# A graph layer in fp32 halves on one Trainium2 core: three row blocks instead of two share the features while these are made

## The chip, the cores and the metric

The kernel runs on one core of a Trainium2 chip. The metric is the device time of one execution in microseconds (us), as the median of the runs shown. The engines are named as in the profile: PE (matrix products; PEld its weight loads), DVE (vector), ACT (scalar), POOL (GpSimd) and SP (the queue that issues most transfers). PE's sums land in eight accumulator banks of 128 x 512 fp32, the tensor `banks`.

## The reference

```python
h = relu(layernorm(x))                      # x 4096 x 256; layernorm without gain or bias, eps 1e-5
deg = sum(adj, axis=1) + 1e-5               # adj 4096 x 4096, dense fp32
out = (adj / deg) @ h @ W_neigh.T + b_neigh + h @ W_self.T + b_self
result = x + relu(out)                      # fp32, 4096 x 256
```

## The kernel before

The 4096 rows of the result are cut into 8 row blocks of 512 (q = 0 to 7). The sum over neighbours is cut into 16 units of 256 columns of `adj` (u = 0 to 15). So there are 128 units, numbered s = 0 to 127 in the order of the table `order` (line 33). Unit (q, u) needs 512 KB of `adj` and the pair u of feature tiles, h of 256 nodes.

Products are made from halves: a value is split into a rounded high part and the rest. PE forms hi·hi, lo·hi and hi·lo for each unit, 12 matmuls of 128 x 512 (lines 573 to 575), which add up over 16 units in the two banks of the row block (`MAIN`).

What each engine does, each in its own program order:

- **SP** loads unit s into slot s % 4 of the ring `adj_raw` (line 173). It first waits until unit s - 4 has been split by ACT and DVE and, where DVE adds it to the row sums, until that is done. Behind the load of some units it issues a pair of x tiles (`load_x`, line 163).
- **ACT** makes the high part of unit s ("hi", line 292). At unit `make_at[p]` it also makes h of pair p (`make_h`, line 295), which waits for POOL's `shift` and `rstd`, and at `split_at[p]` its high part.
- **DVE** makes the low part of unit s ("lo", line 434), and at unit `norm_at[p]` the mean and variance of pair p ("statistics", lines 397 and 401), for which it waits for that pair's x. Then it adds the unit into `total`, from which the degrees come ("add", line 446; a copy, line 443, for the first of a row block). Before the first unit that uses a pair it makes the low part of its h (line 426).
- **POOL** turns variance and mean of a pair into `rstd` and `shift` with four small operations (lines 214, 216, 225, 222). It also issues 14 transfers that add units of q = 0 and 1 into `total_dma` in memory, so that DVE need not add those (`by_dma`, lines 38 and 239).

The slots of the rings are reused after four units, so hi and lo of unit s also wait until PE has used unit s - 4.

While h is being made, units of row blocks 0 and 1 alternate (units 0 to 31): each new pair of h serves two units. After that a row block is 16 units in a row, with h complete.

For each row block there is a second part. `turn` transposes the block's own h (8 transposes, line 590) into two banks, ACT and DVE split that, and `own_product` (24 matmuls, line 599) multiplies it by W_self. `weigh` multiplies the finished sum by W_neigh (24 matmuls), after ACT and DVE have split it (`product_high`, line 351; `product_low`, line 469). `sum_degrees` (line 623) sums the degrees over partitions with four tiny matmuls, from `sums`, which DVE joins (lines 453 and 458); `degrees` (line 474) and `join_rows` (line 483) on DVE, relu on ACT, and `add_bias` (line 247) and `add_x` (line 253) on POOL finish the rows. At which unit each of these stands in each engine's program is written in tables (lines 45 to 56).

The eight banks: two pairs for the sums of even and odd row blocks, one pair for the small products (`SMALL`), one for the transposed h and the degrees (`TURNED`, `SUMMED`). At the end the last block's rows take banks 4, 5, 0, 1.

Of the kernel before, what the change touches and what calls it, by code (L numbers as in the profile page):

```python
# [5 lines left out]
P = 128  # L6
# [15 lines left out]
def gnn_layer(nc, x, adj, wn, ws, bn, bs, out):  # L22
# [23 lines left out]
    own_at = [36, 47, 57, 66] + [16 * q + 11 for q in range(4, Q)]  # L46
    weigh_at = [38, 49, 59, 68] + [16 * (q + 1) + 2 for q in range(4, Q)]
    degrees_at = [w + 1 for w in weigh_at[:-1]]

    product_at = [32, 42, 52] + [last_unit[q] + 3 for q in range(3, Q)]  # L50
# [4 lines left out]
    split_at = [0, 1, 3] + [2 * p - 1 for p in range(3, PAIRS - 1)] + [2 * PAIRS - 4]  # L55
    sums_at = [38, 45, 54, 64] + last_unit[4:]

    with ExitStack() as ctx:
# [91 lines left out]

        MAIN = [[0, 1], [2, 3]]
        SMALL = [4, 5]
        TURNED = [6, 7]
        SUMMED = 7

        TAIL = [4, 5, 0, 1]

        block = ctx.enter_context(nc.Block())

        @block.sync  # L160
        def _(sp):
# [24 lines left out]
            load_unit(3)  # L186
            load_x(3)
            for s in range(RING, S):
                load_unit(s)
                if s % 2 == 0 and s // 2 + 2 < PAIRS:  # L190
                    load_x(s // 2 + 2)
                if s == 9:
                    sp.dma_start(w_raw[:, :, 0, :], wn).then_inc(s_w, 16)
                if s == 11:
                    sp.dma_start(w_raw[:, :, 1, :], ws).then_inc(s_w, 16)
                if s == 13:
# [12 lines left out]
        def _(pool):  # L209
# [57 lines left out]
            for s in range(S):  # L267
# [3 lines left out]
                for n in range(len(by_dma)):  # L271
                    if s == 5 * n // 2 + 5:
                        add_unit(n)
                for q in range(Q):
                    if s == own_at[q] + 5 and q < Q - 1:
                        add_bias(q)
                    if s == weigh_at[q] + 7 and q < Q - 1:
                        add_x(q)
# [7 lines left out]
        def _(act):  # L286
# [41 lines left out]
            def turned_high(q):  # L328
                if q >= 1:
                    act.wait_ge(s_own, 2 * q)  # L330
                for k in range(KC):
                    act.wait_ge(s_turned, 2 * q + k + 1)
                    nc.scalar.activation(ht_hi[:, k, :], banks[:, TURNED[k], :], ACT.Copy).then_inc(s_hthi, 1)

# [8 lines left out]
            def product_high(q):  # L343
                if q >= 1:
                    act.wait_ge(s_weighed, 2 * q)
                for k in range(KC):
                    if k == 0:
                        act.wait_ge(s_half, q + 1)
                    else:
                        act.wait_ge(s_used, last_unit[q] + 1)  # L350
                    nc.scalar.activation(p_hi[:, k, :], banks[:, MAIN[q % 2][k], :], ACT.Copy).then_inc(s_phi, 1)  # L351

# [10 lines left out]
            for s in range(1, S):  # L363
                split_unit(s)
                for p in range(1, PAIRS):
                    if s == make_at[p]:
                        make_h(p)
                    if s == split_at[p]:
                        split_h(p)
                if s == 29:  # L370
                    act.wait_ge(s_w, 32)
                    nc.scalar.activation(w_hi[:, :, :, :], w_raw[:, :, :, :], ACT.Copy).then_inc(s_whi, 1)
                for q in range(Q):
# [4 lines left out]
                    if s == own_at[q] + 4:  # L378
                        take_own(q)
                    if s == product_at[q]:  # L380
                        product_high(q)
                    if s == weigh_at[q] + 6:
                        relu(q)
# [10 lines left out]
        def _(dve):  # L394
# [65 lines left out]
            def turned_low(q):  # L460
                for k in range(KC):
                    dve.wait_ge(s_hthi, 2 * q + k + 1)
                    nc.vector.tensor_tensor(ht_lo[:, k, :], banks[:, TURNED[k], :], ht_hi[:, k, :].bitcast(F32),
                                            ALU.subtract).then_inc(s_htlo, 1)

            def product_low(q):
                for k in range(KC):
                    dve.wait_ge(s_phi, 2 * q + k + 1)
                    nc.vector.tensor_tensor(p_lo[:, k, :], banks[:, MAIN[q % 2][k], :], p_hi[:, k, :].bitcast(F32),
                                            ALU.subtract).then_inc(s_plo, 1)  # L470

            def degrees(q):
                dve.wait_ge(s_summed, q + 1)
                nc.vector.tensor_scalar(deg[:, 0, :], banks[:, SUMMED, 0:UI], DEG_EPS, None, ALU.add).then_inc(s_deg, 1)  # L474
                dve.wait_ge(s_deg, q + 1)
# [25 lines left out]
            for s in range(2, S):  # L501
                if s < T and (s % 2 == 0 and s < T - 2 or s == T - 3):
                    split_h(order[s][1])
# [4 lines left out]
                if by_vector[s]:  # L508
                    add_unit(s)
                if s == 30:  # L510
                    dve.wait_ge(s_whi, 1)
# [4 lines left out]
                for q in range(Q):  # L516
                    if s == turn_at[q] + 4:
                        turned_low(q)
                    if s == product_at[q]:
                        product_low(q)  # L520
                    if s == sums_at[q]:
                        join_sums(q)
                    if s == weigh_at[q] + 4:
                        degrees(q)
# [17 lines left out]
        def _(pe):  # L542
# [16 lines left out]
            def add_unit(s):  # L559
                q, u = order[s]  # L560
                r = s % RING
                if s < T:
                    pe.wait_ge(s_hlo, u + 1)
                if u == 0 and q >= 2:
                    pe.wait_ge(s_plo, 2 * (q - 1))
                pe.wait_ge(s_lo, s + 1)
                for k in range(KC):
                    bank = banks[:, MAIN[q % 2][k], :]
                    feats = slice(k * P, (k + 1) * P)
# [10 lines left out]
            def turn(q):  # L580
# [3 lines left out]
                else:  # L584
                    pe.wait_ge(s_htlo, 2 * q)
                if q >= 1:
                    pe.wait_ge(s_deg, q)
                for k in range(KC):
                    for t in range(UI):
                        last = nc.tensor.transpose(banks[:, TURNED[k], t * P:(t + 1) * P],  # L590
                                                   h_row[:, t // 2, t % 2, k * P:(k + 1) * P], ident[:, :])
# [22 lines left out]
            def sum_degrees(q):  # L614

                pe.wait_ge(s_sums, q + 1)
                pe.wait_ge(s_htlo, 2 * q + 2)
                if q == 0:
                    pe.wait_ge(s_ones, 1)
                else:  # L620
                    pe.wait_ge(s_deg, q)
                for t in range(UI):
                    last = nc.tensor.matmul(banks[:, SUMMED, t:t + 1], sums[:, t * P:(t + 1) * P], ones[:, :],  # L623
                                            start=True, stop=True)
# [27 lines left out]
            for s in range(1, S):  # L652
# [3 lines left out]
                for q in range(Q):  # L656
                    if s == turn_at[q]:
                        turn(q)
                    if s == own_at[q]:
                        own_product(q)  # L660
                    if s == weigh_at[q]:
                        weigh(q)
# [36 lines left out]
```

## Time and profile before

| | |
|---|---|
| median of 3 runs | 438.15 us (436.0 to 438.83) |
| the profiled execution | 436.03 us |
| its span | 434.0 us |
| PE busy in the span | 419.2 us (97%) |
| DVE busy | 360.0 us (83%) |
| ACT busy | 208.0 us (48%) |
| POOL busy | 113.7 us (26%) |
| moved by transfers | 83.98 MB, mean 194 GB/s |

The span runs from the first to the last instruction that counts; the 2 us between span and time lie around it. PE's busy time is an upper bound, since the ends of its matmuls are modelled and overlap; the step from one start to the next is the surer measure, and the times between a wait and the next start are real.

### The profile page before, as it was taken

What the parts mean: (1) busy time and instruction counts of PE and PEld (TensorE: products, weight loads), DVE (VectorE), ACT (ScalarE), POOL (GpSimd) and SP (SyncE); (2) the same over time, 40 slices, a digit from 0 to 9 for tenths busy, and PEclk for the clock granted to TensorE, in tenths of its full rate; (3) what the DMA queues carried; (4) which work ended last, traced back from release to release, by engine and by line L of the source; (5) the groups of instructions that cost most, each with busy time, mean ns of one, the idle gap of its engine ahead of it and who ended that gap; (6) DMA issues with size and microseconds to landing.
All of it is one profiled execution on the core that took longest, in us unless ns stands there. A gap on an engine that the chain in (4) does not pass through costs nothing.

```text
span 434.0 us, 5622 instructions
## 1 busy us (share of the span) xinstructions
PE 419.2 (97%) x2057; PEld 350.7 (81%) x2057; DVE 360.0 (83%) x421; ACT 208.0 (48%) x267; POOL 113.7 (26%) x107
## 2 busy tenths in 40 slices
PE   7799999988999999999999999999999999999995
PEld 4578877766888888888888888888888888888884
DVE  5688888989899896996797796979878897869934
ACT  4675555556533733734442544435342643426411
POOL 4365676741020303432203202002110302003021
PEclk9989999999999999999999999999999999999999
DMA  8779999999945474465347364545745465453501
GB/s 281 250 236 316 310 308 287 290 233 287 272 152 195 145 231 158 142 225 166 109 136 239 127 209 154 192 145 160 242 141 194 138 205 183 146 194 101 189 2 48
DMA packets 25482, 83.98 MB, mean 194 GB/s; under 512 B 2800, under 2 KB 4336, under 8 KB 25456
## 3 DMA queue, kind: packets, MB, share of 16 engines
q1 hardware_dynamic: 22864, 75.64, 52.0%
q0 software_dynamic: 2016, 7.34, 8.3%
q10 hardware_dynamic: 576, 0.66, 0.5%
q8 instruction: 16, 0.26, 0.3%
q14 instruction: 10, 0.08, 0.1%
HBM read 79.43 MB, written 4.19 MB: 193 GB/s over the span
## 4 chain that ended last, share of the span: by engine, by line
PE 74%; DVE 8%; POOL 8%; ACT 4%; issue 3%; DMA 3%; DVEq 0%; POOLq 0%; ACTq 0%; SPq 0%
PE banks L573 20%; PE banks L574 20%; PE banks L575 20%; PE banks L599 10%; DVE adj_lo L434 3%; POOL rstd L216 3%; POOL shift L225 2%; ACT adj_hi L292 2%; DMA adj_raw<-adj_in 2%; POOL rstd L214 2%; DVE total L446 2%; PE banks L590 2%; PE banks L623 1%; ACT h_row L295 1%; DVE stats L397 1%
## 5 line engine op out<-in xcount | busy, mean ns | idle before, releaser
L573 PE MATMUL banks<-adj_hi,h_hi 128*128 128x512 f32 x508 | 201.5, 397 | 7.6 <-DVE adj_lo L434 6.0
L292 ACT ACTIVATE adj_hi<-adj_raw 128x1024 fp32r<-128x1024 f32 x127 | 133.9, 1057 | 146.9 <-PE banks L575 128.2
L575 PE MATMUL banks<-adj_lo,h_hi 128*128 128x512 f32 x508 | 198.6, 391 | 0.0
L574 PE MATMUL banks<-adj_hi,h_lo 128*128 128x512 f32 x508 | 198.6, 391 | 0.0
L434 DVE TENSOR_TENSOR adj_lo<-adj_raw,adj_hi 128x1024 fp32r<-128x1024 f32 x127 | 167.4, 1318 | 35.4 <-ACT adj_hi L292 34.9
L446 DVE TENSOR_TENSOR total<-total,adj_raw 128x1024 f32<-128x1024 f32 x106 | 131.1, 1237 | 0.0
L573 PEld LDWEIGHTS banks<-adj_hi,h_hi 128*128 128x128 f32 x508 | 95.8, 189 | 31.5 <-issue 10.5
L575 PEld LDWEIGHTS banks<-adj_lo,h_hi 128*128 128x128 f32 x508 | 95.7, 188 | 20.6
L574 PEld LDWEIGHTS banks<-adj_hi,h_lo 128*128 128x128 f32 x508 | 95.9, 189 | 18.4
L253 POOL TENSOR_TENSOR x_sb<-x_sb,own 128x1024 f32<-128x1024 f32 x7 | 29.1, 4161 | 135.3 <-ACT own L355 135.3
L247 POOL TENSOR_TENSOR own<-own,b_sum 128x1024 f32<-128x1024 f32 x8 | 22.6, 2823 | 116.8 <-ACT own L340 116.8
L295 ACT ACTIVATE h_row<-x_sb,shift,rstd 128x256 f32<-128x256 f32 x62 | 32.9, 591 | 32.0 <-POOL shift L222 32.0
L474 DVE TENSOR_SCALAR deg<-banks 128x4 f32<-128x4 f32 x8 | 1.3, 162 | 22.0 <-PE banks L623 22.0
L351 ACT ACTIVATE p_hi<-banks 128x512 fp32r<-128x512 f32 x16 | 9.2, 597 | 20.3 <-PE banks L575 14.1
L599 PE MATMUL banks<-w_hi,ht_lo 128*128 128x256 f32 x64 | 18.1, 283 | 0.0
L599 PE MATMUL banks<-w_lo,ht_hi 128*128 128x256 f32 x64 | 18.1, 283 | 0.0
L599 PE MATMUL banks<-w_hi,ht_hi 128*128 128x256 f32 x64 | 18.1, 282 | 0.0
L216 POOL TENSOR_TENSOR rstd<-rstd,consts 128x2 f32<-128x2 f32 (+1 forms) x17 | 17.3, 1017 | 1.3
L214 POOL TENSOR_TENSOR rstd<-mv,consts 128x2 f32<-128x2 f32 (+1 forms) x17 | 10.5, 617 | 27.2 <-DVE mv L401 27.2
L239 POOL DMA_DIRECT2D total_dma<-adj_in x12 | 10.7, 891 | 22.0 <-PE banks L575 17.7
L599 PE MATMUL banks<-w_hi,p_lo 128*128 128x256 f32 x56 | 15.8, 283 | 0.0
L599 PE MATMUL banks<-w_lo,p_hi 128*128 128x256 f32 x56 | 15.8, 283 | 0.0
(65 smaller groups left out, 288.0 us busy)
## 6 DMA issues: line engine op xcount, KB each, us to landing
adj_raw<-adj_in SPq DMA_DIRECT2D x127, 512.0 KB, 4.0
total_dma<-adj_in POOLq DMA_DIRECT2D x14, 512.0 KB, 7.9
x_sb<-x_in SPq DMA_DIRECT2D x14, 256.0 KB, 6.0
rows_out<-x_sb SPq DMA_DIRECT2D x7, 512.0 KB, 5.0
adj_raw<-adj_in SPq DMA_DIRECT2D x2, 256.0 KB, 4.5
x_sb<-x_in ACTq DMA_DIRECT2D x1, 256.0 KB, 4.2
w_raw<-w_neigh SPq DMA_DIRECT2D x1, 256.0 KB, 5.4
w_raw<-w_self SPq DMA_DIRECT2D x1, 256.0 KB, 6.1
```

The costliest lines, as they stand in the source:

```text
L214: nc.gpsimd.tensor_tensor(rstd[:, cols], mv[:, cols, 1], consts[:, 0, 0:n], ALU.add).then_inc(s_rstd, 1)
L216: nc.gpsimd.tensor_tensor(rstd[:, cols], rstd[:, cols], consts[:, 1, 0:n], ALU.pow).then_inc(s_rstd, 1)
L247: nc.gpsimd.tensor_tensor(own[:, :, :], own[:, :, :], b_sum[:, :, :].broadcast_to([P, UI, F]), ALU.add) \
L253: nc.gpsimd.tensor_tensor(x_sb[:, rows, :], x_sb[:, rows, :], own[:, :, :], ALU.add).then_inc(s_final, 1)
L292: nc.scalar.activation(adj_hi[:, r, :, :], adj_raw[:, r, :, :], ACT.Copy).then_inc(s_hi, 1)
L295: return nc.scalar.activation(slot, x_sb[:, t, :], ACT.Relu, bias=shift[:, t:t + 1], scale=rstd[:, t:t + 1])
L434: nc.vector.tensor_tensor(adj_lo[:, r, :, :], adj_raw[:, r, :, :], adj_hi[:, r, :, :].bitcast(F32), ALU.subtract).then_inc(s_lo, 1)
L446: nc.vector.tensor_tensor(total[:, q % 3, :, :], total[:, q % 3, :, :], adj_raw[:, s % RING, :, :], ALU.add).then_inc(s_add, 1)
L573: nc.tensor.matmul(bank, h_hi[:, j, feats], adj_hi[:, r, a, :], start=first, stop=False)
L574: nc.tensor.matmul(bank, h_lo[:, j, feats], adj_hi[:, r, a, :], start=False, stop=False)
L575: done = nc.tensor.matmul(bank, h_hi[:, j, feats], adj_lo[:, r, a, :], start=False, stop=last)
L599: last = nc.tensor.matmul(bank, m[:, k, cols], w[:, k, which, :], start=(n == 0), stop=(n == len(terms) - 1))
```

## The change

Row blocks 0, 1 and 2 now take turns while h is made (units 0 to 47), so each new pair of h serves three units. Three sums are open at once; with row block 3 it is four, so `MAIN` gives banks 0 to 7 to row blocks 0 to 3 and reuses banks 2, 3 and 6, 7 afterwards. The small products then take banks 0 and 1, which are free once row block 0 has been split, and the transposed h takes 0 and 1 for two blocks and 4 and 5 later. The turns, own products and weights of all blocks therefore stand behind unit 48. The tables for x loads, statistics, making and splitting h, `by_dma` transfers and the second part of each block are rewritten for that; `by_dma` names the same 14 units.

```diff
-    order = [(s % 2, s // 2) for s in range(2 * U - 4)] + [(q, u) for q in range(2) for u in range(U - 2, U)]
-    order += [(s // U, s % U) for s in range(2 * U, S)]
+    order = [(s % 3, s // 3) for s in range(3 * U - 6)] + [(q, u) for q in range(3) for u in range(U - 2, U)]
+    order += [(s // U, s % U) for s in range(3 * U, S)]
...
-    turn_at = [32, 43, 53, 62] + [16 * q + 8 for q in range(4, Q)]
+    turn_at = [50, 61, 71, 78, 86, 96, 104, 120]
+    degrees_at = [49, 60] + [w + 1 for w in weigh_at[2:]]
...
-    norm_at = [0, 0, 2, 3] + [2 * p - 4 for p in range(4, PAIRS)]
-    make_at = [0, 1, 3] + [2 * p - 2 for p in range(3, PAIRS - 1)] + [2 * PAIRS - 5]
+    norm_at = [0, 0, 2, 4] + [3 * p - 5 for p in range(4, PAIRS)]
+    make_at = [0, 1] + [3 * p - 3 for p in range(2, PAIRS - 1)] + [first_use[-1] - 2]
...
-        MAIN = [[0, 1], [2, 3]]
-        SMALL = [4, 5]
-        TURNED = [6, 7]
-        SUMMED = 7
-        TAIL = [4, 5, 0, 1]
+        MAIN = [[0, 1], [2, 3], [4, 5], [6, 7], [2, 3], [6, 7], [2, 3], [6, 7]]
+        EARLIER = [None, None, None, None, 1, 3, 4, 5]
+        SMALL = [0, 1]
+        TURNED = [[0, 1]] * 2 + [[4, 5]] * (Q - 2)
+        SUMMED = [0, 0] + [5] * (Q - 2)
+        TAIL = [0, 1, 2, 3]
...
-                if s % 2 == 0 and s // 2 + 2 < PAIRS:
-                    load_x(s // 2 + 2)
+                if s % 3 == 2 and 5 < s and (s + 4) // 3 < PAIRS:
+                    load_x((s + 4) // 3)
...
-                pool.wait_ge(s_used, 5 * n // 2 + 2)
+                pool.wait_ge(s_used, 3 * n + 2)
...
-                    if s == weigh_at[q] + 4:
+                    if s == degrees_at[q] + 3:
                         degrees(q)
...
-                if q >= 1:
+                if q == 0:
+                    pe.wait_ge(s_deg, 1)
+                elif q == 1:
+                    pe.wait_ge(s_joined, 1)
+                    pe.wait_ge(s_deg, 2)
+                else:
+                    pe.wait_ge(s_plo, 6)
                     pe.wait_ge(s_deg, q)
```

How instructions move, at three places. First DVE, while h is made. Before, from the statistics of pair 10 to those of pair 11 (units 16 to 18; `adj_lo` is lo, `total` the add, `h_lo` the low part of h, `mv` ends the statistics):

```order
L397 BN_STATS stats<-x_sb 128x6 [waits x_pair_loaded10]
L397 BN_STATS stats<-x_sb 128x6
L401 BN_AGGR mv<-stats 128x2 [waits stats_done]
L401 BN_AGGR mv<-stats 128x2
L446 TENSOR_TENSOR total<-total,adj_raw 128x1024 [waits unit_added]
L434 TENSOR_TENSOR adj_lo<-adj_raw,adj_hi 128x1024 [waits adj_unit_used,adj_hi_ready]
L426 TENSOR_TENSOR h_lo<-h_row,h_hi 128x512 [waits h_hi_ready]
L434 TENSOR_TENSOR adj_lo<-adj_raw,adj_hi 128x1024 [waits adj_unit_used,adj_hi_ready]
L397 BN_STATS stats<-x_sb 128x6 [waits x_pair_loaded11]
```

Now, from the statistics of pair 6 to those of pair 7 (units 13 to 16); between those of pairs 7 and 8 stand two more adds, one ahead of the first lo and one behind the second:

```order
L400 BN_STATS stats<-x_sb 128x6 [waits x_pair_loaded6]
L400 BN_STATS stats<-x_sb 128x6
L404 BN_AGGR mv<-stats 128x2 [waits stats_done]
L404 BN_AGGR mv<-stats 128x2
L437 TENSOR_TENSOR adj_lo<-adj_raw,adj_hi 128x1024 [waits adj_unit_used,adj_hi_ready]
L449 TENSOR_TENSOR total<-total,adj_raw 128x1024 [waits unit_added]
L429 TENSOR_TENSOR h_lo<-h_row,h_hi 128x512 [waits h_hi_ready]
L437 TENSOR_TENSOR adj_lo<-adj_raw,adj_hi 128x1024 [waits adj_unit_used,adj_hi_ready] x2
L400 BN_STATS stats<-x_sb 128x6 [waits x_pair_loaded7]
```

The statistics of neighbouring pairs were two units apart and are now three apart.

Second PE, around the first `turn`. Before, behind unit 32:

```order
L573 MATMUL banks<-adj_hi,h_hi 128x512
L574 MATMUL banks<-adj_hi,h_lo 128x512
L575 MATMUL banks<-adj_lo,h_hi 128x512
L590 MATMUL banks<-ident,h_row 128x128 [waits ident_ready,h_again_ready]
L590 MATMUL banks<-ident,h_row 128x128 x7
L573 MATMUL banks<-adj_hi,h_hi 128x512 [waits adj_lo_ready]
```

Now, behind unit 50:

```order
L578 MATMUL banks<-adj_hi,h_hi 128x512
L579 MATMUL banks<-adj_hi,h_lo 128x512
L580 MATMUL banks<-adj_lo,h_hi 128x512
L602 MATMUL banks<-ident,h_row 128x128 [waits degree_step_done,ident_ready,h_again_ready]
L602 MATMUL banks<-ident,h_row 128x128 x7
L578 MATMUL banks<-adj_hi,h_hi 128x512 [waits adj_lo_ready]
```

The turn now also waits for `degree_step_done`, the first step of `degrees` on DVE (L477 below). There it stands behind lo and add of unit 52, here from the lo of unit 51 on:

```order
L437 TENSOR_TENSOR adj_lo<-adj_raw,adj_hi 128x1024 [waits adj_unit_used,adj_hi_ready]
L449 TENSOR_TENSOR total<-total,adj_raw 128x1024 [waits unit_added]
L437 TENSOR_TENSOR adj_lo<-adj_raw,adj_hi 128x1024 [waits adj_unit_used,adj_hi_ready]
L449 TENSOR_TENSOR total<-total,adj_raw 128x1024 [waits unit_added]
L477 TENSOR_SCALAR deg<-banks 128x4 [waits degrees_summed]
L479 RECIPROCAL deg<-deg 128x4 [waits degree_step_done]
```

So PE's turn behind unit 50 now waits for DVE's work on unit 52.

Third SP, where x pairs (L163, now L166) are issued among the loads of units. Before, a pair behind every second unit:

```order
L173 DMA adj_raw<-adj_in 128x1024 [waits unit_added,adj_lo_ready,adj_hi_ready] x2
L163 DMA x_sb<-x_in 128x512
L173 DMA adj_raw<-adj_in 128x1024 [waits adj_lo_ready,adj_hi_ready] x2
L163 DMA x_sb<-x_in 128x512
L173 DMA adj_raw<-adj_in 128x1024 [waits unit_added,adj_lo_ready,adj_hi_ready] x2
```

Now a pair behind every third:

```order
L176 DMA adj_raw<-adj_in 128x1024 [waits unit_added,adj_lo_ready,adj_hi_ready]
L166 DMA x_sb<-x_in 128x512
L176 DMA adj_raw<-adj_in 128x1024 [waits unit_added,adj_lo_ready,adj_hi_ready] x2
L176 DMA adj_raw<-adj_in 128x1024 [waits adj_lo_ready,adj_hi_ready]
L166 DMA x_sb<-x_in 128x512
```

x of pair p was issued behind the load of unit 2p - 4, whose lo stands just ahead of that pair's statistics on DVE. It is now issued behind the load of unit 3p - 4, one unit later than the one (3p - 5) behind which its statistics stand.

## Rows read from the trace of the kernel before

**Rows 1.** The page, part 1: busy time, share of the span, instructions.

```profile
PE 419.2 (97%) x2057; PEld 350.7 (81%) x2057; DVE 360.0 (83%) x421; ACT 208.0 (48%) x267; POOL 113.7 (26%) x107
```

**Rows 2.** PE in order of time: start us, us, instruction, [idle before <- releaser].

```profile
10.50 0.47 PE L573 MATMUL banks<-adj_hi,h_hi 128*128 128x512 f32 x1 [0.19 <-DVE adj_lo L434]
...
35.12 0.39 PE L573 MATMUL banks<-adj_hi,h_hi 128*128 128x512 f32 x1
...
37.84 0.39 PE L573 MATMUL banks<-adj_hi,h_hi 128*128 128x512 f32 x1
...
109.59 1.03 PE L590 MATMUL banks<-ident,h_row 128*128 128x128 f32 x8
110.38 0.48 PE L573 MATMUL banks<-adj_hi,h_hi 128*128 128x512 f32 x1
```

**Rows 3.** The chain of waits, one loop: start us, us, work.

```profile
56.87 0.67 DVE stats L397 x2
...
57.90 1.08 POOL rstd L214
...
59.05 1.58 POOL rstd L216
60.63 1.23 POOL shift L225
...
61.99 0.20 POOL shift L222
...
62.73 0.59 ACT h_row L295
...
68.40 0.67 DVE stats L397 x2
```

**Rows 4.** DVE in order of time, the same loop, and unit 7.

```profile
29.29 1.28 DVE L434 TENSOR_TENSOR adj_lo<-adj_raw,adj_hi 128x1024 fp32r<-128x1024 f32 x1 [1.56 <-ACT adj_hi L292]
...
56.78 0.74 DVE L397 BATCH_NORM_STATS2 stats<-x_sb 128x6 f32<-128x256 f32 x2
...
57.73 1.19 DVE L446 TENSOR_TENSOR total<-total,adj_raw 128x1024 f32<-128x1024 f32 x1
58.83 1.22 DVE L434 TENSOR_TENSOR adj_lo<-adj_raw,adj_hi 128x1024 fp32r<-128x1024 f32 x1
59.97 0.68 DVE L426 TENSOR_TENSOR h_lo<-h_row,h_hi 128x512 fp32r<-128x512 f32 x1
60.58 1.22 DVE L434 TENSOR_TENSOR adj_lo<-adj_raw,adj_hi 128x1024 fp32r<-128x1024 f32 x1
...
64.30 1.23 DVE L434 TENSOR_TENSOR adj_lo<-adj_raw,adj_hi 128x1024 fp32r<-128x1024 f32 x1 [1.56 <-ACT adj_hi L292]
```

**Rows 5.** POOL in order of time, the other half of the loops.

```profile
51.62 0.47 POOL L214 TENSOR_TENSOR rstd<-mv,consts 128x2 f32<-128x2 f32 x1
...
54.19 0.99 POOL L222 TENSOR_TENSOR shift<-shift,rstd 128x2 f32<-128x2 f32 x1
```

**Rows 6.** DVE in order of time, work that stands once or once per row block.

```profile
99.32 1.22 DVE L512 TENSOR_TENSOR w_lo<-w_raw,w_hi 128x1024 fp32r<-128x1024 f32 x1
...
104.79 0.69 DVE L443 COPY total<-adj_raw 128x1024 f32<-128x1024 f32 x1
105.39 1.28 DVE L469 TENSOR_TENSOR p_lo<-banks,p_hi 128x512 fp32r<-128x512 f32 x2
...
126.07 3.43 DVE L446 TENSOR_TENSOR total<-total,adj_raw 128x1024 f32<-128x1024 f32 x1
...
140.03 1.66 DVE L483 SCALAR_TENSOR_TENSOR own<-banks,deg,own 128x256 f32<-128x256 f32 x4
```

**Rows 7.** The page, part 6, transfers: issue, count, KB each, median us to landing.

```profile
x_sb<-x_in SPq DMA_DIRECT2D x14, 256.0 KB, 6.0
```

**Rows 8.** The chain of waits behind 120 us: one own product.

```profile
121.52 2.87 PE banks L599 x24
```

**Rows 9.** POOL in order of time, behind 120 us.

```profile
125.60 2.82 POOL L247 TENSOR_TENSOR own<-own,b_sum 128x1024 f32<-128x1024 f32 x1 [11.08 <-ACT own L340]
```

More of the change, by code:

```diff
@@ L41, in gnn_layer @@
     first_added = [min(s for s in range(S) if order[s][0] == q and by_vector[s]) for q in range(Q)]
-    turn_at = [32, 43, 53, 62] + [16 * q + 8 for q in range(4, Q)]
[L46 to L50, printed above, removed]
-    norm_at = [0, 0, 2, 3] + [2 * p - 4 for p in range(4, PAIRS)]
-    make_at = [0, 1, 3] + [2 * p - 2 for p in range(3, PAIRS - 1)] + [2 * PAIRS - 5]
-    split_at = [0, 1, 3] + [2 * p - 1 for p in range(3, PAIRS - 1)] + [2 * PAIRS - 4]
-    sums_at = [38, 45, 54, 64] + last_unit[4:]
+    first_use = [min(s for s in range(S) if order[s][1] == p) for p in range(PAIRS)]
+    turn_at = [50, 61, 71, 78, 86, 96, 104, 120]
+    own_at = [53, 64, 74, 82, 90, 99, 107, 123]
+    weigh_at = [55, 66, 76, 84, 92, 101, 114]
+    degrees_at = [49, 60] + [w + 1 for w in weigh_at[2:]]
+    product_at = [46, 58, 69, 79, 87, 98, 114]
+    sums_at = [47, 56, 66, 81, 88, 97, 111, 127]
+    norm_at = [0, 0, 2, 4] + [3 * p - 5 for p in range(4, PAIRS)]
+    make_at = [0, 1] + [3 * p - 3 for p in range(2, PAIRS - 1)] + [first_use[-1] - 2]
+    split_at = [0, 1] + [3 * p - 2 for p in range(2, PAIRS - 1)] + [first_use[-1] - 1]
     with ExitStack() as ctx:
@@ L276, in _ @@
                         add_bias(q)
-                    if s == weigh_at[q] + 7 and q < Q - 1:
+                    if q < Q - 1 and s == weigh_at[q] + 7:
                         add_x(q)
@@ L332, in turned_high @@
                     act.wait_ge(s_turned, 2 * q + k + 1)
-                    nc.scalar.activation(ht_hi[:, k, :], banks[:, TURNED[k], :], ACT.Copy).then_inc(s_hthi, 1)
+                    nc.scalar.activation(ht_hi[:, k, :], banks[:, TURNED[q][k], :], ACT.Copy).then_inc(s_hthi, 1)
             def take_own(q):
@@ L350, in product_high @@
                         act.wait_ge(s_used, last_unit[q] + 1)
-                    nc.scalar.activation(p_hi[:, k, :], banks[:, MAIN[q % 2][k], :], ACT.Copy).then_inc(s_phi, 1)
+                    nc.scalar.activation(p_hi[:, k, :], banks[:, MAIN[q][k], :], ACT.Copy).then_inc(s_phi, 1)
             def relu(q):
@@ L379, in _ @@
                         take_own(q)
-                    if s == product_at[q]:
+                    if q < Q - 1 and s == product_at[q]:
                         product_high(q)
-                    if s == weigh_at[q] + 6:
+                    if q < Q - 1 and s == weigh_at[q] + 6:
                         relu(q)
@@ L462, in turned_low @@
                     dve.wait_ge(s_hthi, 2 * q + k + 1)
-                    nc.vector.tensor_tensor(ht_lo[:, k, :], banks[:, TURNED[k], :], ht_hi[:, k, :].bitcast(F32),
+                    nc.vector.tensor_tensor(ht_lo[:, k, :], banks[:, TURNED[q][k], :], ht_hi[:, k, :].bitcast(F32),
                                             ALU.subtract).then_inc(s_htlo, 1)
@@ L468, in product_low @@
                     dve.wait_ge(s_phi, 2 * q + k + 1)
-                    nc.vector.tensor_tensor(p_lo[:, k, :], banks[:, MAIN[q % 2][k], :], p_hi[:, k, :].bitcast(F32),
+                    nc.vector.tensor_tensor(p_lo[:, k, :], banks[:, MAIN[q][k], :], p_hi[:, k, :].bitcast(F32),
                                             ALU.subtract).then_inc(s_plo, 1)
@@ L473, in degrees @@
                 dve.wait_ge(s_summed, q + 1)
-                nc.vector.tensor_scalar(deg[:, 0, :], banks[:, SUMMED, 0:UI], DEG_EPS, None, ALU.add).then_inc(s_deg, 1)
+                nc.vector.tensor_scalar(deg[:, 0, :], banks[:, SUMMED[q], 0:UI], DEG_EPS, None, ALU.add).then_inc(s_deg, 1)
                 dve.wait_ge(s_deg, q + 1)
@@ L501, in _ @@
             for s in range(2, S):
-                if s < T and (s % 2 == 0 and s < T - 2 or s == T - 3):
+                if s in first_use:
                     split_h(order[s][1])
@@ L509, in _ @@
                     add_unit(s)
-                if s == 30:
+                if s == 46:
                     dve.wait_ge(s_whi, 1)
@@ L518, in _ @@
                         turned_low(q)
+                    if s == sums_at[q]:
+                        join_sums(q)
+                    if q == Q - 1:
+                        continue
                     if s == product_at[q]:
                         product_low(q)
-                    if s == sums_at[q]:
-                        join_sums(q)
-                    if s == weigh_at[q] + 4:
+                    if s == degrees_at[q] + 3:
                         degrees(q)
@@ L561, in add_unit @@
                 r = s % RING
-                if s < T:
+                if s < 3 * U:
                     pe.wait_ge(s_hlo, u + 1)
-                if u == 0 and q >= 2:
-                    pe.wait_ge(s_plo, 2 * (q - 1))
+                if u == 0 and q >= 4:
+                    pe.wait_ge(s_plo, 2 * (EARLIER[q] + 1))
                 pe.wait_ge(s_lo, s + 1)
                 for k in range(KC):
-                    bank = banks[:, MAIN[q % 2][k], :]
+                    bank = banks[:, MAIN[q][k], :]
                     feats = slice(k * P, (k + 1) * P)
@@ L589, in turn @@
                     for t in range(UI):
-                        last = nc.tensor.transpose(banks[:, TURNED[k], t * P:(t + 1) * P],
+                        last = nc.tensor.transpose(banks[:, TURNED[q][k], t * P:(t + 1) * P],
                                                    h_row[:, t // 2, t % 2, k * P:(k + 1) * P], ident[:, :])
@@ L616, in sum_degrees @@
                 pe.wait_ge(s_sums, q + 1)
-                pe.wait_ge(s_htlo, 2 * q + 2)
                 if q == 0:
+                    pe.wait_ge(s_plo, 2)
                     pe.wait_ge(s_ones, 1)
+                elif q == 1:
+                    pe.wait_ge(s_joined, 1)
                 else:
+                    pe.wait_ge(s_htlo, 2 * q + 2)
                     pe.wait_ge(s_deg, q)
                 for t in range(UI):
-                    last = nc.tensor.matmul(banks[:, SUMMED, t:t + 1], sums[:, t * P:(t + 1) * P], ones[:, :],
+                    last = nc.tensor.matmul(banks[:, SUMMED[q], t:t + 1], sums[:, t * P:(t + 1) * P], ones[:, :],
                                             start=True, stop=True)
@@ L660, in _ @@
                         own_product(q)
-                    if s == weigh_at[q]:
+                    if q < Q - 1 and s == weigh_at[q]:
                         weigh(q)
```

10 lines of the change are left out of this document (5 added, 5 removed).

## The prediction, made before the run

> **What bounds the kernel now.** I read the busy times first. PE is busy for 419.2 of 434.0 us [rows 1], so 15 us at most are to be had, and the question is where PE stands still. The timeline of PE answers it. A unit takes 2.72 us from start to start when nothing is missing (35.12 to 37.84) [rows 2]. Unit 1 starts at 10.50. The first turn, behind unit 32, is over when unit 33 starts at 110.38; in between lie 32 units of 2.72, that is 87.0, and the turn of 0.8 (109.59 to 110.38) [rows 2]. The stretch is 99.9 us long, so PE waited 12.0 us in it. From there to the last unit the starts follow each other without a gap. All that can be gained lies in the first 110 us; behind them PE's work alone counts, and the change leaves that work as it is.
>
> What PE waits for there is read from the chain of waits, which shows one pattern again and again: DVE's statistics of a pair, four small POOL operations (57.90 to 62.19), ACT's h (to 63.32), then hi and lo of the next unit, and from there new statistics, 56.87 to 68.40, 11.53 us [rows 3]. That is a loop: the statistics of pair p hold back h of pair p, h stands ahead of a hi in ACT's program, and that hi's lo stands ahead of later statistics. The loop of before covers four units, which PE does in 10.88 us. It is too long by 0.65 us. The POOL operations are long for two columns of data because they wait for DVE: the second ends at 60.63, with DVE's h_lo (59.97 + 0.68) [rows 3, 4].
>
> **The change part by part.** I name DVE's steps by the distance of starts [rows 4]: lo 1.14 (58.83 to 59.97), add the same within 0.04 (57.73 to 58.83), h_lo 0.61, the statistics of a pair 0.95 (56.78 to 57.73).
>
> (1) The loop. It now runs from the statistics of pair p at unit 3p - 5 over h at 3p - 3, which holds hi of 3p - 2, to the statistics of pair p + 1 behind lo of 3p - 2. It covers three units, 8.16 us of PE. In even loops DVE's program behind the statistics is lo, add, h_lo, lo: four operations as long as those of the measured loop. There, from the end of the statistics (57.73) to the start of the lo that was held (64.30), it took 6.57 us [rows 4]. With lo and new statistics that is 6.57 + 1.14 + 0.95 = 8.66. In odd loops two more adds stand there, and DVE alone has three lo, three adds, h_lo and the statistics: 6 x 1.13 + 0.61 + 0.95 = 8.34. That is the longest part there: by the measured pattern POOL gets a turn at each end of a DVE operation, so its four end with the third add and h_lo, ACT needs 2 us more, and the held hi is ready about when DVE comes to it. From pair 4 to pair 15 there are 6 even and 5 odd loops: 6 x 8.66 + 5 x 8.34 = 93.7 us for 33 units, where PE needs 89.8.
>
> (2) The start. The measured lo of unit 7 ends, for the next operation, at 29.29 + 1.14 = 30.4 [rows 4]. In the new order pair 3 is made for unit 9, not 6, but the same chain of two loops leads to unit 7; one half less stands ahead of it. I take 29.5, with 1 us to each side. Lo of unit 40, the last that carries a loop, then ends at 123.2 and the statistics of pair 15 at 124.1.
>
> (3) The last pair and the way to the first turn. Add 40, lo and add 41 and h_lo 14 take DVE 4.0 us. Hi 42 is held by h of pair 15 until 6.25 us behind the statistics (the four POOL operations between DVE's four, 4.2; h 1.0; hi 1.0). Then DVE has lo 42 to 52 (11), ten adds and a copy, h_lo 15, the low half of the weights with the bias (99.32 to about 100.8, 1.5), one p_lo (1.2) [rows 6], the joined degree sums (an add and a half, 1.7) and the first step of the degrees (0.2): 12.5 + 11.3 + 0.6 + 0.6 + 1.5 + 1.2 + 1.7 + 0.2 = 29.6. So the turn, which now waits for that step, can start at 124.1 + 6.25 + 29.6 = 160.0 (rounded up). All these adds are DVE's, since no unit behind u = 12 is added by a transfer. PE's own work from 10.50 to there is 50 units and the degree sums, 136.1 us. Its waits sum to 160.0 - 10.5 - 136.1 = 13.4 us, where they were 12.0. The edit costs 1.4 us here, with the 1 us of (2) to each side: the loops' waits are not shorter in total, and DVE, which has no room in front of the turn, ends the rest.
>
> (4) The x pairs. In even loops x is issued behind a load that waits for an add; that is 1.13 + 0.4 us behind the previous statistics, and its own statistics are due 8.34 - 0.95 = 7.4 us behind these. There is room for 5.9 us, and the median landing takes 6.0 [rows 7]. Before, four units' time lay between. If x comes 0.4 us late in each of five such loops that costs 2.0 us, since DVE then stands in front of the statistics with adds and lo's queued behind them, and SP's loads behind those. From below it costs nothing (x in 4 us, as in an idle stretch); from above 6 us (1.2 us late each time). I take 2.0, near the median.
>
> (5) The second parts. They keep their instructions; 24 matmuls take 2.87 us as before [rows 8] and lie on PE in either order. New is that the turns of blocks 0, 1, 3 and 4 wait for a degree step that DVE has two units later than PE has the turn. Behind the first turn I follow both for block 1. PE: turn, three units, own product, two units, weigh: 20.2 us; six more units and the degree sums: 36.7. DVE is held at unit 58 by p_lo until that weigh ends, since ACT's p_hi waits for it; lo 59 starts at 22.3, and five units, the joined rows (1.66) [rows 6] and the degree step need 11.4 + 1.7 + 0.2. With a POOL addition on the way, beside which an add took 3.43 us where it takes 1.2 [rows 6, 9], that is 37.8. PE waits 1.1 us. For block 3 the same account leaves DVE 1 us ahead, for block 4 level. I take 1.5 us for all of them, 0 to 3.5.
>
> (6) At no cost: the banks (each is split before it is written again, by DVE's own order: p_lo of the earlier block stands ahead of the lo that unit waits for); the rows stored, which stand twelve units behind weigh as before; the tail, where only bank numbers differ. The cover is PE's lead of two to three units behind the first turn; without it each of these waits would show in full, which the upper end of (5) holds.
>
> The sum against the profiled execution: 436.03 + 1.4 + 2.0 + 1.5 = 440.9 us. The median of the runs lies 2.1 us above this execution, so against it the forecast is 438.15 + 4.9 = 443.0 (rounded).
>
> **The rivals.** *POOL is quicker, and the change gains.* In the other half of the loops before, the four operations took 51.62 to 55.18, 3.6 us, not 4.3 [rows 5], since DVE stood still beside them. If they do so here, even loops fall by 0.7 to 7.95 us and the eleven loops to 89.4, under PE's 89.8. Their excess of 3.9 us is gone, h of pair 15 comes 0.7 us sooner, and with no late x, no wait at the later turns and the start 1 us earlier the sum is 1.4 - 3.9 - 0.7 - 1.0 = -4.2: some 434 us against the median. It decides from the point where an even loop is shorter than 8.0. Against it: the measured loop with four such DVE operations behind its statistics is the long one.
>
> *Nothing is late that is not late already.* With x on time and PE ahead at the later turns only the 1.4 us of (3) stay, or 2.4 with a late start: 439.5 to 440.5 against the median, no difference. For it: the loops per unit are as long as before, 8.5 / 3 = 2.83 against 11.53 / 4 = 2.88.
>
> *One more wait for POOL.* In odd loops POOL meets six DVE operations with no gap between them. The measured loop shows its operations ending with one of DVE's, and cannot tell whether the second needs one end or two, since a short h_lo followed there [rows 3, 4]. If it needs two, h comes 1.1 us later and the five odd loops are 9.4 long: 5 x 1.07 = 5.3 us more, 448 us. The Trainium skill ("SBUF — State Buffer", section "Who interferes with whom") says that a DVE instruction with two inputs in SBUF and a POOL instruction that reads SBUF exclude each other for whole instructions; by that rule a POOL operation that just misses an end waits for a whole DVE operation more, which speaks for this rival, and the ends in the trace agree with it.
>
> **How the numbers follow.** A measurement of this kernel tells about 1% from no change, that is 4.4 us. I give the forecast, 441 to 446, 0.40; nothing late, 0.28; one more wait or x later than assumed, 446 to 451, 0.20; the gain, 0.12. The forecast's case lies about the limit of 442.5: three quarters of it count as slower, with the third rival's 0.20 and a little of the second's. So slower 0.52, same 0.37, faster 0.11. The range goes from 435 (most of the gain's case left out) to 450.
>
> **What would show each step.** Right: statistics of neighbouring pairs 8.3 to 8.8 us apart between 30 and 124 us, with PE's gaps ended by lo; a gap at unit 42 of 2 to 3 us ended by DVE, from ACT, from POOL; a PE wait for DVE at the first turn, which starts at 158 to 166 us; a second one at the turn of block 1; no gap behind 300 us. Wrong: loops at or under 8.16 us, PE without gaps behind unit 10; or PE waiting on transfers (hi of a unit late by a landing), which I have only in x; or a longer tail.

## The result and the profile after

The changed kernel takes 439.36 us (median of 12 runs, 438.3 to 442.1), the kernel before beside it 436.99 us (12 runs, 434.9 to 438.83). The ratio is 1.0062 [1.0036, 1.0088]: slower by 0.6%, some 2.4 to 2.7 us, which is under the 1% that the prediction set as a difference. The forecast was 4.9 us and 443.0.

The profiled execution took 440.38 us, its span is 438.3. That is 1.0 us above the median, and the profiled execution of the kernel before (436.03) is 1.0 us below its own; between the two profiles are 4.35 us. The page's busy times, to be held against [rows 1]:

```profile
PE 421.4 (96%) x2057; PEld 349.9 (80%) x2057; DVE 355.7 (81%) x421; ACT 207.0 (47%) x267; POOL 119.4 (27%) x107
```

Each engine's instructions are the same in number. POOL is busier by 5.7 us, with no more to do. The waits say why; first those of the kernel before (engine, line waited for, us in total, times, longest):

```profile
ACT h_row L295 <- POOL shift L222: 32.0, 12, 4.6
PE banks L573 <- DVE adj_lo L434: 6.0, 8, 1.9
```

and of the changed kernel:

```profile
ACT h_row L298 <- POOL shift L225: 45.4, 13, 4.8
PE banks L578 <- DVE adj_lo L437: 9.1, 15, 2.1
DVE stats L400 <- DMA x_sb<-x_in: 3.8, 3, 2.3
```

ACT waits 13.4 us longer for POOL and, through it, PE 3.1 us longer for lo. The last unit starts 4.3 us later than before (427.80 for 423.49): 0.9 us of that is that unit 1 started later (11.38 for the 10.50 of [rows 2]), 3.0 us are lost between unit 1 and the first turn, 0.4 us behind it.

The chain of waits of the changed kernel, one even loop, which answers to [rows 3]:

```profile
28.74 0.67 DVE stats L400 x2
...
29.78 1.08 POOL rstd L217
...
30.93 1.58 POOL rstd L219
32.50 1.23 POOL shift L228
...
34.60 0.59 ACT h_row L298
35.19 0.96 ACT adj_hi L295
36.17 1.23 DVE adj_lo L437
37.40 0.67 DVE stats L400 x2
```

From 28.74 to 37.40 are 8.66 us, to the hundredth the forecast of an even loop. By the starts of the statistics in DVE's timeline the eleven loops from pair 4 to pair 15 are 8.65, 8.34, 8.66, 8.33, 9.96, 8.34, 8.66, 9.13, 8.67, 8.34 and 9.45, in sum 96.5 us (forecast 93.7). Three fall out of the pattern. Two of them end with an x that came late, in the same chain:

```profile
64.01 8.57 DMA x_sb<-x_in
72.60 0.76 DVE stats L400 x2
...
92.58 6.13 DMA x_sb<-x_in
98.73 0.77 DVE stats L400 x2
```

The third is the last. POOL and DVE in order of time:

```profile
116.86 1.07 POOL L217 TENSOR_TENSOR rstd<-mv,consts 128x2 f32<-128x2 f32 x1 [3.43 <-DVE mv L404]
118.00 1.58 POOL L219 TENSOR_TENSOR rstd<-rstd,consts 128x2 f32<-128x2 f32 x1
119.56 1.24 POOL L228 TENSOR_TENSOR shift<-mv,consts 128x2 f32<-128x2 f32 x1
120.95 0.99 POOL L225 TENSOR_TENSOR shift<-shift,rstd 128x2 f32<-128x2 f32 x1
```

```profile
116.68 1.19 DVE L437 TENSOR_TENSOR adj_lo<-adj_raw,adj_hi 128x1024 fp32r<-128x1024 f32 x1
117.79 1.22 DVE L449 TENSOR_TENSOR total<-total,adj_raw 128x1024 f32<-128x1024 f32 x1
118.92 0.69 DVE L429 TENSOR_TENSOR h_lo<-h_row,h_hi 128x512 fp32r<-128x512 f32 x1
119.53 1.22 DVE L437 TENSOR_TENSOR adj_lo<-adj_raw,adj_hi 128x1024 fp32r<-128x1024 f32 x1
120.66 1.22 DVE L449 TENSOR_TENSOR total<-total,adj_raw 128x1024 f32<-128x1024 f32 x1
124.05 1.23 DVE L437 TENSOR_TENSOR adj_lo<-adj_raw,adj_hi 128x1024 fp32r<-128x1024 f32 x1 [2.16 <-ACT adj_hi L295]
```

Each POOL operation ends with one of DVE's: 117.93 with 117.87, 119.58 with 119.61, 120.80 with 120.75, 121.94 with 121.88. The last add (120.66) is of a unit behind u = 12, which no transfer adds; in the even loops before it DVE stood idle there and the fourth operation took 0.2 us (33.86 in the chain above). That is the 0.8 us of this loop.

The way to the first turn, PE in order of time:

```profile
11.38 0.47 PE L578 MATMUL banks<-adj_hi,h_hi 128*128 128x512 f32 x1 [1.22 <-DVE adj_lo L437]
...
133.74 0.47 PE L578 MATMUL banks<-adj_hi,h_hi 128*128 128x512 f32 x1 [2.12 <-DVE adj_lo L437]
...
159.08 0.95 PE L638 MATMUL banks<-ones,sums 128*128 128x1 f32 x8
...
163.35 1.07 PE L602 MATMUL banks<-ident,h_row 128*128 128x128 f32 x8 [0.45 <-DVE deg L477]
...
201.35 1.07 PE L602 MATMUL banks<-ident,h_row 128*128 128x128 f32 x8 [0.23 <-DVE deg L477]
```

The gap at unit 42 (133.74) and the waits for the degree step at the turns of blocks 0 and 1 are where they were looked for. Between 11.38 and 163.35 lie 50 units of 2.72 (136.0), the degree sums (0.95) and hence 15.0 us of waits.

Some 1.7 us of these 15.0 are slow matmuls and not waits. Right behind the gap of 2.12 us at unit 42 the granted clock is 0.54 from 134.6 to 138.0, near the lower of TensorE's two levels (1.2 of 2.4 GHz), and matmuls start 0.43 us apart instead of 0.23. The kernel before has the same behind a gap of 1.95 us (clock 0.50 from 24 to 26), so 1.7 of the prediction's 12.0 us are no waits either, and the difference between the two kernels is not touched.

One more transfer was late on this way, a load. In the chain of waits, and then in DVE's order of time:

```profile
134.81 7.23 DMA adj_raw<-adj_in
```

```profile
143.16 1.22 DVE L437 TENSOR_TENSOR adj_lo<-adj_raw,adj_hi 128x1024 fp32r<-128x1024 f32 x1 [1.01 <-ACT adj_hi L295]
```

That is unit 46, and from there to the turn's degree step DVE works without a gap, so its 1.01 us are in the first turn.

### The profile page after: what moved, and what is told of

Read it like the earlier page. It is cut to its first block, busy times and chain, and to the rows that moved or that the text cites. A ratio compares the mean times of both kernels' runs of the same rounds, so it can differ in the third digit from the quotient of the medians.

```text
span 438.3 us, 5643 instructions
## 1 busy us (share of the span) xinstructions
PE 421.4 (96%) x2057; PEld 349.9 (80%) x2057; DVE 355.7 (81%) x421; ACT 207.0 (47%) x267; POOL 119.4 (27%) x107
## 4 chain that ended last, share of the span: by engine, by line
PE 62%; DVE 15%; POOL 7%; DMA 6%; issue 4%; ACT 4%; SPq 1%; DVEq 0%; POOLq 0%; ACTq 0%
PE banks L578 17%; PE banks L580 16%; PE banks L579 16%; PE banks L611 10%; DVE adj_lo L437 5%; DVE total L449 5%; DMA x_sb<-x_in 4%; POOL rstd L219 3%; ACT adj_hi L295 2%; DVE stats L400 2%; PE banks L602 2%; DMA adj_raw<-adj_in 2%; ACT h_row L298 2%; POOL rstd L217 2%; POOL shift L228 2%
## 5 line engine op out<-in xcount | busy, mean ns | idle before, releaser
L437 DVE TENSOR_TENSOR adj_lo<-adj_raw,adj_hi 128x1024 fp32r<-128x1024 f32 x127 | 164.0, 1291 | 43.8 <-ACT adj_hi L295 43.1
L449 DVE TENSOR_TENSOR total<-total,adj_raw 128x1024 f32<-128x1024 f32 x106 | 128.8, 1215 | 0.0
L256 POOL TENSOR_TENSOR x_sb<-x_sb,own 128x1024 f32<-128x1024 f32 x7 | 26.9, 3849 | 109.8 <-ACT own L358 109.8
L217 POOL TENSOR_TENSOR rstd<-mv,consts 128x2 f32<-128x2 f32 (+1 forms) x17 | 14.6, 859 | 57.1 <-DVE mv L404 57.1
L219 POOL TENSOR_TENSOR rstd<-rstd,consts 128x2 f32<-128x2 f32 (+1 forms) x17 | 23.7, 1396 | 1.3
L472 DVE TENSOR_TENSOR p_lo<-banks,p_hi 128x512 fp32r<-128x512 f32 x16 | 10.4, 686 | 12.5 <-ACT p_hi L354 12.5
L611 PE MATMUL banks<-w_hi,p_hi 128*128 128x256 f32 x56 | 15.8, 282 | 0.0
```

Source lines behind the costliest of these rows:

```text
L217: nc.gpsimd.tensor_tensor(rstd[:, cols], mv[:, cols, 1], consts[:, 0, 0:n], ALU.add).then_inc(s_rstd, 1)
L219: nc.gpsimd.tensor_tensor(rstd[:, cols], rstd[:, cols], consts[:, 1, 0:n], ALU.pow).then_inc(s_rstd, 1)
L256: nc.gpsimd.tensor_tensor(x_sb[:, rows, :], x_sb[:, rows, :], own[:, :, :], ALU.add).then_inc(s_final, 1)
L437: nc.vector.tensor_tensor(adj_lo[:, r, :, :], adj_raw[:, r, :, :], adj_hi[:, r, :, :].bitcast(F32), ALU.subtract).then_inc(s_lo, 1)
L449: nc.vector.tensor_tensor(total[:, q % 3, :, :], total[:, q % 3, :, :], adj_raw[:, s % RING, :, :], ALU.add).then_inc(s_add, 1)
L611: last = nc.tensor.matmul(bank, m[:, k, cols], w[:, k, which, :], start=(n == 0), stop=(n == len(terms) - 1))
```

## The experiments

Two theories. *The loop theory*: statistics, POOL, h, hi and lo close on themselves within three units, the loop is longer than PE's 8.16 us, and what PE loses it loses there. *The transfer theory*: x and the loads come late, among the transfers that add to `total_dma`, and the loop only looks like the cause. Each kernel ran in five rounds against the kernel before, whose median was 436.1 to 436.2 us.

**x issued sooner (e1_x_early).**

```diff
-                if s % 3 == 2 and 5 < s and (s + 4) // 3 < PAIRS:
-                    load_x((s + 4) // 3)
+                if s % 3 == 0 and 3 < s and (s + 6) // 3 < PAIRS:
+                    load_x((s + 6) // 3)
```

> The changed kernel with one edit: x of pair p is issued behind the load of unit 3p - 6 instead of 3p - 4. Loop theory (the waits of PE's first stretch come from the loop statistics, POOL, h, hi, lo, lengthened where x lands late): the two long x waits in the changed kernel's chain (8.57 and 6.13 us from issue to landing) go, the loops stay at 8.34 to 8.66 us, time falls by 1 to 2.5 us, to 437 to 438.5. Transfer theory (the transfers as such set the stretch, whatever their order): no change, 439 to 440, since x only takes the place of unit loads.

439.37 us, 1.0070 [1.0049, 1.0092]: nothing gained. DVE waits for x once only, at the kernel's start; the loops are 8.66 and 8.34 but for two of 8.9 and the last. That one is 10.20, 0.75 more than in the changed kernel, since now a unit's load came late (chain of waits):

```profile
114.50 8.91 DMA adj_raw<-adj_in
123.43 1.07 ACT adj_hi L295
```

In this profile the lateness moved to another transfer. The price of the late x was not to be had in this way.

**The statistics one unit sooner (e2_stats_early).** With the same edit of x, and

```diff
-    norm_at = [0, 0, 2, 4] + [3 * p - 5 for p in range(4, PAIRS)]
+    norm_at = [0, 0, 2, 4] + [3 * p - 6 for p in range(4, PAIRS)]
```

> As the run with x early, and the statistics of pair p one unit earlier on DVE (3p - 6), so that they stand ahead of the lo that h of the pair before holds back. Loop theory: the loop now needs two pairs, six units, and no longer binds; units 7 to 40 go at PE's 2.72 us or nearly, 5 to 6 us less than the 96.5 of the changed kernel's profile, and DVE has a lead at the first turn: 432 to 435 us. Transfer theory: as the run with x early, 437 to 440.

431.29 us, 0.9906 [0.9875, 0.9937], 8 us less than the changed kernel, less than the kernel before, and less than the 432 to 435 expected. The statistics now stand in front of the lo that the loop holds, so the chain no longer closes within one pair. Since x alone (e1) gave nothing, the gain is that of the statistics' step, for which x has to be there sooner. The waits:

```profile
ACT h_row L298 <- POOL shift L225: 13.1, 6, 4.0
PE banks L578 <- DVE adj_lo L437: 3.1, 6, 1.1
```

The eleven loops sum to 88.3 us, under PE's 89.8, with single ones between 6.7 and 10.2. ACT, which stood still for POOL, now does so for loads: between 20 and 130 us it waits 34.6 us for them, where it waited 13.2. One place in its timeline, first the changed kernel, then this one:

```profile
86.38 1.09 ACT L298 ACTIVATE h_row<-x_sb,shift,rstd 128x256 f32<-128x256 f32 x2 [2.95 <-POOL shift L225]
```

```profile
84.80 1.06 ACT L295 ACTIVATE adj_hi<-adj_raw 128x1024 fp32r<-128x1024 f32 x1 [2.42 <-DMA adj_raw<-adj_in]
```

The first turn comes at 153.53 instead of 163.35:

```profile
153.53 1.07 PE L602 MATMUL banks<-ident,h_row 128*128 128x128 f32 x8 [0.40 <-DVE deg L477]
```

**No adding transfers (e3_no_adding_transfers).** The changed kernel without 12 of its 14 transfers into `total_dma`; the degrees of blocks 0 and 1 lack those units.

```diff
-                    pool.wait_ge(s_dadd[q], 16 * (n // 2))
-                    pool.dma_start(total_dma[:, q, :, :], adj[q, u, :, :, :], accum_op=ALU.add).then_inc(s_dadd[q], 16)
+                    return
...
-                    dve.wait_ge(s_dadd[q], 16 * (len(by_dma) // 2))
+                    dve.wait_ge(s_dadd[q], 16)
```

> The changed kernel without the 12 transfers that add a unit into total_dma (the first two stay), so the degrees of row blocks 0 and 1 lack these units; nothing else is left out. 6.3 MB and their descriptors less in the first 130 us. Loop theory: loops stay at 8.3 to 8.7 us, only late x and late raw go: 437 to 438.5. Transfer theory: the first stretch loses most of its waits, 5 us or more: 434 or less.

438.21 us, 1.0039 [1.0016, 1.0061], 1.2 us less than the changed kernel and than e1. The loops stay, now without a miss: 8.66, 8.34 in turn, 9.45 the last. An odd loop in the chain (line numbers are one lower here):

```profile
55.46 0.68 DVE stats L399 x2
...
63.80 0.67 DVE stats L399 x2
```

This tells the theories apart: without this traffic the loops stand as they were. What all lateness from it costs the changed kernel is some 1.2 us by the medians (the two intervals overlap); the load of unit 46 holds DVE up no longer either.

**The same step in the kernel before (e4_before_stats_early).**

```diff
-    norm_at = [0, 0, 2, 3] + [2 * p - 4 for p in range(4, PAIRS)]
+    norm_at = [0, 0, 2, 3] + [2 * p - 5 for p in range(4, PAIRS)]
...
+            load_x(4)
...
-                if s % 2 == 0 and s // 2 + 2 < PAIRS:
-                    load_x(s // 2 + 2)
+                if s % 2 == 1 and (s + 5) // 2 < PAIRS:
+                    load_x((s + 5) // 2)
```

> The kernel before with x and statistics of each pair from 4 on one unit earlier (2p - 5). Loop theory: the loop of before, 11.53 us for four units, loses a lo, an add or an h_lo (0.6 to 1.2 us) and comes to PE's 10.88 or under; the waits of units 16 to 27 go, about 2 us, those at units 28 to 32 stay if they are landings: 434 to 435.5 against 437.0. Transfer theory: no change, 436 to 438.

433.98 us, 0.9950 [0.9925, 0.9975], 2.1 us less: the kernel before was held by its loop too. ACT's wait for POOL falls from 32.0 to 5.0 us. With the loop open in both, three blocks (431.29) stand 2.7 us below two (433.98). The two intervals overlap slightly, so this gain of the change is likely rather than certain.

**h one unit later (e7_h_late).** The loop opened at its other end: h behind the hi that it held, x and statistics as in the changed kernel.

```diff
-    make_at = [0, 1] + [3 * p - 3 for p in range(2, PAIRS - 1)] + [first_use[-1] - 2]
-    split_at = [0, 1] + [3 * p - 2 for p in range(2, PAIRS - 1)] + [first_use[-1] - 1]
+    make_at = [0, 1, 3, 6] + [3 * p - 2 for p in range(4, PAIRS - 1)] + [first_use[-1] - 2]
+    split_at = [0, 1, 4, 7] + [3 * p - 1 for p in range(4, PAIRS - 1)] + [first_use[-1] - 1]
```

> The changed kernel with x and statistics where they were, and h of pairs 4 to 14 made and split one unit later on ACT (3p - 2 and 3p - 1): h then holds back the hi behind the next statistics, not the one ahead of them. Loop theory: it opens the same loop from the other side, so statistics come at 8.2 us or less but for late x (2 to 4 us in all), and the time falls by 4 to 8 us, to 431.5 to 435.5. Transfer theory: no change, 439.

434.49 us, 0.9967 [0.9951, 0.9983], 4.9 us less than the changed kernel with every transfer as it was. PE has no gap from unit 6 to 41; the next one is that of the last pair, whose h was not moved:

```profile
126.75 0.50 PE L578 MATMUL banks<-adj_hi,h_hi 128*128 128x512 f32 x1 [2.00 <-DVE adj_lo L437]
```

**No adding transfers, loop open (e6_early_no_adding).** The edits of e2 and e3 together; the degrees lack the same units.

> The run with statistics early, without the 12 transfers that add into total_dma (the degrees of row blocks 0 and 1 lack these units; nothing else is left out). Loop theory: with the loop open the landings are what is left in units 7 to 40, so here, unlike in the changed kernel itself (1.2 us), they should go: the two intervals of statistics of 10.20 and 9.60 us fall to about 8.2; but DVE's work from 46 on stays, so 429 to 431. Transfer theory: 5 us or more, 426 or less.

428.21 us, 0.9819 [0.9806, 0.9832]. The same edit that gave 1.2 us with the loop closed gives 3.1 with it open, and the four runs lie within 0.2 us where the twelve of e2 spread over 5.5. The time lies between what the two theories expected: the transfer theory, wrong for the changed kernel, names the next limit.

**Two tries at that limit.** The weights split at units 29 and 30 instead of 45 and 46 on top of e2 (e5_weights_early):

```diff
-                if s == 45:
+                if s == 29:
...
-                if s == 46:
+                if s == 30:
```

> The run with statistics early, and the low half of the weights with the bias sum (1.47 us of DVE) at unit 30 instead of 46 (the high half on ACT at 29 instead of 45). Loop theory: units 7 to 40 now have DVE time to spare, and from unit 46 to the first turn DVE works without a gap, so the first turn starts about 1.5 us earlier and the time is 429.5 to 430.5. Transfer theory (what is left in the first turn's start is set by landings): no change, 431 to 432.

431.83 us, 0.9916 [0.9885, 0.9947]: a miss, nothing gained, as the transfer theory had it. DVE's freed time is lost again at unit 46, whose load took 7.88 us (chain of waits, then DVE in order of time):

```profile
125.58 7.88 DMA adj_raw<-adj_in
```

```profile
134.58 1.23 DVE L437 TENSOR_TENSOR adj_lo<-adj_raw,adj_hi 128x1024 fp32r<-128x1024 f32 x1 [1.62 <-ACT adj_hi L295]
```

So, on top of that, two adding transfers fewer, and two adds more on DVE (e8_fewer_adding):

```diff
-    by_dma = [(0, 0), (1, 0)] + [(1 - u % 2, u) for u in range(1, U - 3)]
+    by_dma = [(0, 0), (1, 0)] + [(1 - u % 2, u) for u in range(1, U - 5)]
```

> The run with weights early, with 12 transfers that add into total_dma instead of 14, so the last is issued at unit 38 and not at 44; DVE adds the other two units (2.3 us, at units 33 and 36, where it has time). If the weights' 1.5 us did not show because raw 46 landed late behind the last two adding transfers (7.88 us from issue in that run's trace, lo 46 held 1.6 us), that landing now comes in 5 us or less and the time is 429 to 431, below the run with statistics early. If DVE's work is the limit there, the two adds cost up to 2.3 us: 432 to 434.

432.59 us, 0.9913 [0.9891, 0.9934]: no gain either. The wait at unit 46 is gone, and the two adds take its place; the first turn stays where e2 had it (153.46 us).

By the medians the best kernel with the whole computation is e2; e5 and e8 cannot be told from it.

## Why the prediction was half right

The sign and the mechanism came out, the amount did not: of 4.9 us about half came, too little to count as slower. The steps that failed are sizes: the degree sums counted as waits in (3), late x in (4) and above all the later turns in (5) were put too high, the last loop in (1) too low, and the difference was taken against the one profiled execution of the kernel before, not its median.

- **(1) The loop** came out to the hundredth: 8.66 and 8.34, and e2 and e7 show from both ends that PE's waits hang on it. Mis-sized was the last loop, counted as an even one. The fifth DVE operation makes it 9.45, 0.8 us that the sum lacked; it is the same in e3, so no transfer makes it.
- **(2) The start** held within its 1 us: the statistics behind lo of unit 7 start at 28.66 in DVE's timeline (forecast 29.5). It moves between executions: in the profiles of e1 and e3 it is 29.73.
- **(3) The way to the first turn** came near in time and was wrong in its account. The turn starts at 163.35; the forecast, with late x, was 162.0. The near agreement is partly luck: the start 0.8 us early against the last loop 0.8 longer, and then 1.0 us at the late load of unit 46, which the forecast does not have, and some 0.35 us more for DVE's work up to the turn. But of this time the text gave PE 136.1 us of work, the degree sums at next to nothing; the profile shows 0.95. The kernel before has them too, only behind its first turn, so they are no cost of the change. The forecast counted some 0.85 us of them as waits: the first failed term, which leaves 0.55 of its 1.4.
- **(4) Late x** was put at 2.0 us. By its own numbers, room for 5.9 us and a landing of 6.0, x is late by 0.1 us a loop and 0.5 in five; the 0.4 that it multiplied comes from no row. In the profile two x were late, by 1.3 us (a landing of 8.57) and, in an odd loop where none was looked for, by 0.8 (an ordinary landing, but issued 3.0 us behind the statistics before). With the load of unit 46 that makes 3.1 us of lateness in this execution. By the medians e3 shows 1.2 us as the price of all that the adding transfers make late, and e1 that issuing x sooner gives nothing back. So the term was some 0.8 us too large for the median, and it named x where any transfer could be the late one.
- **(5) The later turns** were put at 1.5 us. Of the 4.3 us by which the last unit is later, 0.9 lie ahead of unit 1 and 3.0 (15.0 less 12.0) up to the first turn, which leaves 0.4. The turn of block 1 with its unit takes 4.07 us where that of block 2 takes 3.51; 0.14 us of the difference stand right behind the degree sums, and the 0.4 us left is the turn's, 0.23 of it idle in its row, where 1.1 were forecast. The mechanism is the one named, a DVE operation stretched by POOL's addition on the way; but it is a lo of 2.87 us here, 0.6 us less than the add of 3.43 that the forecast took from [rows 6]:

```profile
197.12 2.87 DVE L437 TENSOR_TENSOR adj_lo<-adj_raw,adj_hi 128x1024 fp32r<-128x1024 f32 x1 [0.46 <-ACT adj_hi L295]
...
201.06 0.15 DVE L477 TENSOR_SCALAR deg<-banks 128x4 f32<-128x4 f32 x1
```

```profile
193.30 5.61 POOL L256 TENSOR_TENSOR x_sb<-x_sb,own 128x1024 f32<-128x1024 f32 x1 [13.21 <-ACT own L358]
```

In both places the DVE operation ends 1.08 us behind POOL's (128.42 and 129.50 in [rows 9] and [rows 6], 198.91 and 199.99 here). The stretch is what was left of POOL's operation when DVE's came, 2.35 us there and 1.79 here, so the row of another place did not give its size. That is most of what is missing; the rest stays open.

- **(6) Nothing else** held: no gap behind 300 us, the tail as before.
- **The base.** The median of three, 438.15, was above what more runs gave (436.99 over 12), and the forecast was set on it. That put 1.2 us into 443.0, and none into the difference. But the 4.9 us were worked out against a profiled execution 1.0 us below that median of twelve, and the profile of the changed kernel is 1.0 us above its own.

Together, by the profiles: 4.9 - 0.85 (degree sums) - 0.8 (start) + 1.1 (3.1 late for 2.0) + 0.8 (last loop) + 0.35 (DVE's work) - 1.1 (later turns) = 4.4 us, against 4.35 measured. The profiles alone would have made 4.9 look nearly right, by errors that cancel. With e3's 1.2 us in place of the 3.1 the sum is 2.5 us, against 2.4 to 2.7 by the medians; how far that agreement is luck stays open, since no trace shows a median execution of either kernel. What failed were small terms and the execution they were held against, not the reading of what bounds the kernel.

Of the rivals, the case called nothing late (439.5 to 440.5) lies nearest to the measured time, but in number only: transfers were late, and its base was 1.2 us too high. A quicker POOL fell (no even loop at 7.95), and so did one more wait for POOL: its odd loops of 9.4 are 8.34. What the rule of the Trainium skill ("SBUF — State Buffer", section "Who interferes with whom") says of DVE and POOL excluding each other for whole instructions agrees with the four ends above; a lost turn on top of it is not seen in any loop.

Whether landings can be made shorter with the loop open stays open. e6 shows 3.1 us there, e5 and e8 did not get at them, and between 135 and 153 us DVE has no room for more adds.

## What to carry to other kernels

When a produced item gets more consumers, follow the chain of one item through all engines' programs until it meets itself, and divide its length by the units that it now spans; if that is over the bottleneck's time per unit, move the loop's head in front of the held instruction before adding buffers or reordering consumers. Here one number in a table of positions was worth 8 us (with x issued sooner, which alone gave nothing), the reordering itself at most 3. And count a cost of the change only where the kernel before does not pay the same further on: that error, two generous small terms and a difference taken against one execution instead of the median made a change of little weight into a forecast of slower.

## What was unexpected of the hardware

- Four POOL operations on two columns need 3.9 to 5.1 us beside DVE's two-input operations; in the last loop each ends within 0.06 us of one of DVE's ends. The loops built on it repeat to 0.01 us (e3).
- The degree sums are four matmuls with a single column each (x8 in the row), and yet that row holds PE for 0.95 us.
- How far the runs spread told of transfers: 3.8 us in the changed kernel and 1.3 in e3, 5.5 us in e2 and 0.2 in e6 (four runs). In e3 and e6 only 6.3 MB of adding transfers are missing.
